# A two-layer transformer block on one core: the last batch gets its stacks in other memory

## The reference

```python
x = x + tanh(g_xattn[0]) * L0_xattn(layernorm(x), ctx)   # stage X: 8 heads of 64, 512 keys from ctx
x = x + tanh(g_ffn[0])   * L0_ffn(layernorm(x))          # stage F: 16 heads of 8, 256 keys from x; plus MoE, top 2 of 8
x = x + tanh(g_xattn[1]) * L1_xattn(layernorm(x), ctx)   # stage B: 16 heads of 8, 512 keys from ctx
x = x + tanh(g_ffn[1])   * L1_ffn(layernorm(x))          # stage C: MoE, top 2 of 8
```

## Time and profile before

| | |
|---|---|
| median of 3 runs | 752.22 us (744.86, 756.33, 752.22) |
| the profiled execution's own time | 746.59 us |
| its span, first to last instruction | 744.8 us |
| mean granted clock of PE, as a share of full speed | 0.933 |
| busy: PE, DVE, ACT, POOL | 89%, 76%, 50%, 46% |

### The profile page before, as it was taken

How to read it: one execution, slowest core, us unless ns; L and a number is a source line. 1 busy time by engine, 2 the same in 40 slices (tenths; PEclk the granted TensorE clock), 3 DMA queues, 4 the chain that set the end, 5 groups by cost and what they waited for, 6 DMA issues and landing times.

```text
span 744.8 us, 13302 instructions
## 1 busy us (share of the span) xinstructions
PE 663.1 (89%) x5232; PEld 336.2 (45%) x5232; DVE 569.7 (76%) x1055; ACT 374.2 (50%) x482; POOL 344.5 (46%) x467
## 2 busy tenths in 40 slices
PE   6699898998999899989999999989999789787684
PEld 2265454553544455434645355534653424333342
DVE  2626578589998879788898979887888987928534
ACT  4064345545546753775357644765357346263360
POOL 4273753852463257415663368326764324422233
PEclk9599999999999999989999999999999969969597
DMA  7210202112101221121121311121013221021000
GB/s 193 80 58 19 86 1 62 45 44 63 43 24 41 77 64 52 52 79 32 41 66 42 99 48 65 36 75 50 22 58 97 71 68 68 4 89 55 7 1 14
DMA packets 45790, 40.82 MB, mean 55 GB/s; under 512 B 4824, under 2 KB 37536, under 8 KB 45728
## 3 DMA queue, kind: packets, MB, share of 16 engines
q1 hardware_dynamic: 45168, 39.52, 17.1%
q10 hardware_dynamic: 560, 0.46, 0.2%
HBM read 22.93 MB, written 17.04 MB: 54 GB/s over the span
## 4 chain that ended last, share of the span: by engine, by line
PE 66%; DVE 21%; ACT 6%; issue 2%; POOL 2%; DMA 2%; SPq 1%; POOLq 0%; DVEq 0%
PE psum L670 13%; PE psum L626 7%; PE psum L590 7%; DVE mx8B L925 7%; PE psum L582 6%; DVE mxA L831 4%; PE psum L658 4%; ACT probB L740 4%; PE psum L557 3%; PE psum L639 3%; PE psum L551 3%; PE psum L600 2%; PE psum L577 2%; DVE rden L839 2%; PE psum L675 2%
## 5 line engine op out<-in xcount | busy, mean ns | idle before, releaser
L925 DVE TENSOR_REDUCE mx8B<-psum 128x2 f32<-128x1024 f32 x128 | 153.7, 1219 | 22.7 <-PE psum L639 21.5
L740 ACT ACTIVATE probB<-psum 128x1024 f32<-128x1024 f32 x128 | 126.4, 1029 | 57.2 <-PE psum L658 56.5
L727 ACT ACTIVATE probX<-psum 128x1024 f32<-128x1024 f32 x64 | 65.5, 1024 | 95.1 <-PE psum L582 94.8
L920 DVE TENSOR_REDUCE mx8F<-psum 128x4 f32<-128x1024 f32 x64 | 77.0, 1217 | 8.8 <-PE psum L633 8.6
L831 DVE TENSOR_REDUCE mxA<-psum 128x2 f32<-128x1024 f32 x64 | 76.6, 1216 | 8.5 <-PE psum L564 8.1
L839 DVE RECIPROCAL rden<-psum 128x256 f32<-128x256 f32 x32 | 56.1, 1752 | 34.8 <-PE psum L594 34.7
L740 ACT ACTIVATE probF<-psum 128x1024 f32<-128x1024 f32 x64 | 65.1, 1026 | 24.0 <-PE psum L658 22.2
L999 POOL TENSOR_TENSOR prodC<-prodC 128x256 f32<-128x256 f32 x30 | 21.8, 725 | 104.6 <-DVE prodC L913 102.3
L670 PE MATMUL psum<-probB,v8B 128*32 128x256 f32 x1024 | 67.5, 408 | 2.8 <-ACT probB L740 2.7
L582 PE MATMUL psum<-qX,kX 64*128 64x256 f32 x512 | 68.4, 388 | 0.0
L991 POOL TENSOR_TENSOR psum_k<-probX 128x512 f32<-128x512 f32 x32 | 40.8, 1274 | 59.5 <-ACT probX L727 58.5
(11 more groups left out here) (192 smaller groups left out, 1174.2 us busy)
## 6 DMA issues: line engine op xcount, KB each, us to landing
k8B<-k_dK SPq DMA_DIRECT2D x32, 192.0 KB
k_dK<-partsK SPq DMA_DIRECT2D x8, 384.0 KB, 2.5
q8F<-q_dF SPq DMA_DIRECT2D x32, 96.0 KB
k8F<-k_dF SPq DMA_DIRECT2D x32, 96.0 KB
q8B<-q_dB SPq DMA_DIRECT2D x32, 96.0 KB
k_dK<-partsK SPq DMA_DIRECT2D x8, 256.0 KB, 2.7
cTX<-in_ctxT SPq DMA_DIRECT2D x8, 192.0 KB, 2.8
cTK<-in_ctxT SPq DMA_DIRECT2D x8, 192.0 KB, 2.4
```

What stands on the lines that cost most here:

```text
L727: nc.scalar.activation(prob[s][(8 * b + k) % SLOTS[s]][:], ps, ACT.Exp, scale=float(XD) ** -0.5).then_inc(done["ACT"], 1)
L740: nc.scalar.activation(prob[s][(units * b + k) % SLOTS[s]][:], ps, ACT.Exp, scale=float(D8) ** -0.5).then_inc(done["ACT"], 1)
L920: nc.vector.tensor_reduce(mx8[s][:].rearrange("p t (i q) -> p i t q", i=2)[:, :, :, k], ps.rearrange("p (i t n) -> p i t n", i=2, t=QT), A ...
L925: nc.vector.tensor_reduce(mx8[s][:, t, :].rearrange("p (i q) -> p i q", i=2)[:, :, p], ps.rearrange("p (i n) -> p i n", i=2), AX.X, ALU.ma ...
```

## The change

For the last batch (7) alone:

- K's keys and values are made from `cTX`, the context that stage X loaded for the same batch. The load into `cTK` falls away.
- The queries of B go to `q8F` in place of `q8B`. The first half of the keys goes to `k8F` and the second half to `kXb`. These are free when F's exps and X's maxima of batch 7 are done. The reads into them wait for F's last exp, no longer for B's exps of batch 6.
- POOL sets `kXb` to 1.0 first, in a new job `ones`, for the rows that stay 1.0.
- `mr` of batch 7 doesn't wait for the exps of batch 6.

The way in which the maxima are sent and read (L512, L517) is the same before and after. In the diff, the helper functions `queries`, `keys` and `context` name the new places.

```diff
+LAST = BATCH - 1
@@ plan_stack
+    if s == "K" and b == LAST:
+        p.job("POOL", s, "ones", b, 0, 2.2, ("PE", "X", "mx", b, 7))
     for k in range(2):
-        p.job("SP", s, "sr", b, k, 2.6 if s == "F" else 1.3, ("SP", s, "sw", b, 0), ("PE", *old, b - 1, (4 if s == "F" else 8) * k + 3 + 4 * (s != "F")))
+        free = ("PE", *old, b - 1, (4 if s == "F" else 8) * k + 3 + 4 * (s != "F"))
+        if s != "F" and b == LAST:
+            free = ("POOL", "K", "ones", b, 0) if s == "K" and k else ("PE", "F", "e8", b, NPAIR - 1)
+        p.job("SP", s, "sr", b, k, 2.6 if s == "F" else 1.3, ("SP", s, "sw", b, 0), free)
@@ plan_attend
-    p.job("SP", s, "mr", b, 0, 1.25, ("SP", s, "mw", b, 0), ("PE", s, "e8", b - 1, units - 1))
+    p.job("SP", s, "mr", b, 0, 1.25, ("SP", s, "mw", b, 0), *[("PE", s, "e8", b - 1, units - 1)] * ((s, b) != ("B", LAST)))
@@ plan_k
+def context(b):
+    return "K" if b < LAST else "X"
-    p.job("SP", "K", "ctx", b, 0, .4, ("PE", "K", "kk", b - 1, 0), ("PE", "K", "vv", b - 1, 1))
-    p.fill("ACT", 0, "K", "kk", b, 0, 1.0, 1.4, [("SP", "K", "ctx", b, 0)], [("SP", "K", "sw", b - 1, 0)])
+    if b < LAST:
+        p.job("SP", "K", "ctx", b, 0, .4, ("PE", "K", "kk", b - 1, 0), ("PE", "K", "vv", b - 1, 1))
+    p.fill("ACT", 0, "K", "kk", b, 0, 1.0, 1.4, [("SP", context(b), "ctx", b, 0)], [("SP", "K", "sw", b - 1, 0)])
@@ build
+        def queries(s, b):
+            return q8["F" if (s, b) == ("B", LAST) else s]
+        def keys(s, b, rows, p):
+            if (s, b) != ("B", LAST):
+                return k8[s][rows, p, :]
+            if p < NPAIR // 2:
+                return k8["F"][rows, 2 * p:2 * p + 2, :].rearrange("r o n -> r (o n)")
+            return kXb[rows, p - NPAIR // 2, :]
@@ load_parts
-                sp.wait_ge(*is_full(to, "e8", b - 1, NPAIR * KEYS[to] // SEQ // 2 * (k + 1) - 1))
+                if (to, b) != ("B", LAST):
+                    sp.wait_ge(*is_full(to, "e8", b - 1, NPAIR * KEYS[to] // SEQ // 2 * (k + 1) - 1))
+                else:
+                    sp.wait_ge(*is_full("F", "e8", LAST, NPAIR - 1))
+                    if s == "K" and k:
+                        sp.wait_ge(padded, 1)
@@ mr
-                    sp.wait_ge(*is_full(s, "e8", b - 1, NPAIR * KEYS[s] // SEQ - 1))
+                    if (s, b) != ("B", LAST):
+                        sp.wait_ge(*is_full(s, "e8", b - 1, NPAIR * KEYS[s] // SEQ - 1))
@@ pool
+                if name == "ones":
+                    pool.wait_ge(*is_full("X", "mx", b, 7))
+                    engine.memset(kXb[:], 1.0).then_inc(padded, 1)
```

More of the change, by code:

```diff
@@ L149, in plan_f @@
                 [("DVE", "F", "wb", b, 0), ("POOL", "B", "xb", b - 1, 0), ("DVE", "B", "xh", b - 1, 0)])
+def context(b):
+    return "K" if b < LAST else "X"
 def plan_k(p, b):
-    p.job("SP", "K", "ctx", b, 0, .4, ("PE", "K", "kk", b - 1, 0), ("PE", "K", "vv", b - 1, 1))
-    p.fill("ACT", 0, "K", "kk", b, 0, 1.0, 1.4, [("SP", "K", "ctx", b, 0)], [("SP", "K", "sw", b - 1, 0)])
+    if b < LAST:
+        p.job("SP", "K", "ctx", b, 0, .4, ("PE", "K", "kk", b - 1, 0), ("PE", "K", "vv", b - 1, 1))
+    p.fill("ACT", 0, "K", "kk", b, 0, 1.0, 1.4, [("SP", context(b), "ctx", b, 0)], [("SP", "K", "sw", b - 1, 0)])
     plan_stack(p, "K", b, 3.9, 3, ("ACT", "K", "kk", b, 0), ("B", "e8"))
     for k in range(2):
-        p.fill("DVE", 0, "K", "vv", b, k, .58, .43, [("SP", "K", "ctx", b, 0)], [("PE", "B", "pv8", b - 1, 3)])
+        p.fill("DVE", 0, "K", "vv", b, k, .58, .43, [("SP", context(b), "ctx", b, 0)], [("PE", "B", "pv8", b - 1, 3)])
 def plan_b(p, b):
@@ L403, in build @@
         w_keys, w_values, w_queries, w_ident, zeroed = sem("w_keys"), sem("w_values"), sem("w_queries"), sem("w_ident"), sem("zeroed")
-        picked = sem("picked")
+        picked, padded = sem("picked"), sem("padded")
         def bank(s, name, b, k):
@@ L482, in load_parts @@
                     if s != "K":
-                        engine.dma_start(q8[s][rows, pairs, :].rearrange("r p n -> r (p n)"),
+                        engine.dma_start(queries(s, b)[rows, pairs, :].rearrange("r p n -> r (p n)"),
                                          q_d[s].rearrange("j (i d p) n -> i d j p n", i=2, p=NPAIR)[i, :, :, pairs]
@@ L486, in load_parts @@
                     if s != "B":
-                        engine.dma_start(k8[to][rows, pairs, :].rearrange("r p n -> r (p n)"),
+                        stack = k8[to][rows, pairs, :]
+                        if (to, b) == ("B", LAST):
+                            stack = kXb[rows, :, :] if k else k8["F"][rows, :, :]
+                        engine.dma_start(stack.rearrange("r p n -> r (p n)"),
                                          k_d[s].rearrange("j (i d p) n -> i d j p n", i=2, p=NPAIR)[i, :, :, pairs]
@@ L514, in _ @@
                     sp.wait_ge(*after(s, "mw", b))
-                    sp.wait_ge(*is_full(s, "e8", b - 1, NPAIR * KEYS[s] // SEQ - 1))
+                    if (s, b) != ("B", LAST):
+                        sp.wait_ge(*is_full(s, "e8", b - 1, NPAIR * KEYS[s] // SEQ - 1))
                     for i in range(2):
-                        engine.dma_start(q8[s][64 * i + KROWS:64 * i + MROWS],
+                        engine.dma_start(queries(s, b)[64 * i + KROWS:64 * i + MROWS],
                                          m2_d[s].rearrange("t (i p) n -> i t p n", i=2)[i]).then_inc(S[s]["mr"], 16)
@@ L607, in _ @@
                 elif name == "kk":
-                    pe.wait_ge(*after("K", "ctx", b))
-                    last = mm(ps[:, 0:KV], wk8["B"][:], cT["K"][:, :], start=True, stop=True)
+                    pe.wait_ge(*after(context(b), "ctx", b))
+                    last = mm(ps[:, 0:KV], wk8["B"][:], cT[context(b)][:, :], start=True, stop=True)
                 elif name in ("v8", "vv"):
@@ L613, in _ @@
                     else:
-                        pe.wait_ge(*after("K", "ctx", b))
+                        pe.wait_ge(*after(context(b), "ctx", b))
                     for j in range(2):
                         c = 2 * k + j
-                        tok = xT["F"][:, c * P:(c + 1) * P] if s == "F" else cT["K"][:, c * P:(c + 1) * P]
+                        tok = xT["F"][:, c * P:(c + 1) * P] if s == "F" else cT[context(b)][:, c * P:(c + 1) * P]
                         last = mm(ps[:, j * P:(j + 1) * P], tok, wv8["F" if s == "F" else "B"][:], start=True, stop=True)
@@ L638, in _ @@
                         for i in range(2):
-                            last = mm(ps[:, KV * i:KV * (i + 1)], q8[s][64 * i:64 * i + KROWS, p, t * P:(t + 1) * P],
-                                      k8[s][64 * i:64 * i + KROWS, p, :], start=True, stop=True)
+                            last = mm(ps[:, KV * i:KV * (i + 1)], queries(s, b)[64 * i:64 * i + KROWS, p, t * P:(t + 1) * P],
+                                      keys(s, b, slice(64 * i, 64 * i + KROWS), p), start=True, stop=True)
                 elif name == "mT8":
@@ L658, in _ @@
                             last = mm(ps[:, 512 * i + SEQ * c:512 * i + SEQ * (c + 1)],
-                                      k8[s][64 * i:64 * i + MROWS, p, (c0 + c) * P:(c0 + c + 1) * P],
-                                      q8[s][64 * i:64 * i + MROWS, p, :], start=True, stop=True)
+                                      keys(s, b, slice(64 * i, 64 * i + MROWS), p)[:, (c0 + c) * P:(c0 + c + 1) * P],
+                                      queries(s, b)[64 * i:64 * i + MROWS, p, :], start=True, stop=True)
                 elif name == "pv8":
@@ L964, in _ @@
                     made = True
-                if name == "rs":
+                if name == "ones":
+                    pool.wait_ge(*is_full("X", "mx", b, 7))
+                    engine.memset(kXb[:], 1.0).then_inc(padded, 1)
+                elif name == "rs":
                     pool.wait_ge(*after(s, "mv", b))
```

## The result

The changed kernel takes 764.69 us (median of 4 runs, 763.27 to 765.50); the kernel before takes 749.75 (4 runs, 744.86 to 756.33). The ratio is 1.0162, with a 95% interval of 1.0119 to 1.0205: slower, and the interval reaches just past 2%. The quotient of the two medians is 1.020, and against the 25 later runs of the kernel before (median 753.69, beside E1 to E4) it is 1.015, so the size is known to about half a per cent. The forecast was 762.8 us, and slower by 1.4%.

A forecast was written before the change was run, and what follows sets the result against it. Bound by PE's work from 400 to 560 us, later by the chain inside stage B. Batch 4's milestone 562.0 + periods 116.0 + end 75.1 = 753.1, plus clock 2.3 = 755.4 us of span; median 762.8, range 750 to 775.

The forecast's parts named there:

- The order as the cost: Middle of the program: B's jobs lose priority to X and F from batch 2 on, putting batch 4's milestone 25.5 us late.
- batch 4's lateness: Batch 4's milestone (second copy of `mT8` on DVE) moves from 536.5 to 562.0 us, and later milestones follow.
- X's end: X's last output, 559.5 us before, comes 2.5 us later because F's gate instructions move between `pv` of X's batch 7.
- The periods: From batch 4's milestone to batch 6's: kept at 62.0 + 54.0 = 116.0 us, with ends 87.4 and 124.
- Rival 4: A faster kernel: both periods shrink to 43.7 us, giving 734.2 us as median; chance 0.06.
- Rival 1: Cold end and long periods: all eight `pv8` blocks cold, both periods 62.0 us, giving 777.7 us as median; chance 0.24.
- The end: From batch 6's milestone to the program's end: 75.1 us in place of 92.3.
- The clock: PE's granted clock near the end: two more cold `pv8` blocks, 2.3 us, with 0 and 9.2 as ends.
- The base: Forecast span 755.4 us, 10.6 more; profiled execution 746.6 becomes 757.2, and the median lies 5.6 higher, at 762.8.
- The gain of 17.2 us: Program's end: batch 7's maxima run beside batch 6's HBM way and exps, cutting 92.3 us to 75.1.
- Rival 3: The order costs less: X's end stays, both periods 54.0 us, the clock costs nothing, 750.0 us as median; chance 0.16.
- Rival 2: Stack reads hang behind F's last exp or in SP's queue; the end stays 92.3 us, median 777.7; chance 0.04.

The follow-up runs named there:

- E1: Kernel before, its lists ranked by the changed plan's priorities, with old dependencies, places and waits: 779.41 us, ratio to before 1.0360.
- E4: Changed kernel, with one planner line letting the transpose of batch 4's maxima start without the allowance for drains queued on DVE: 756.63 us, ratio 1.0065.
- E5: Kernel before, with one planner dependency more: the transpose of batch 4's maxima comes behind X's output of batch 7: 783.12 us, ratio 1.0429.
- E11: Changed kernel, with the planner's allowance for queued drains (`LEAD`) at 1.75 in place of 2.0: 761.79 us, ratio 1.0122.
- E2: New places and waits with the lists of the kernel before (one `cTK` load out, the memset in): 751.20 us, ratio 0.9959.
- E7: Changed kernel, with batch 7's keys and values made from their own load of the context again: 763.29 us.
- E8: Changed kernel, with the two matmuls of each of stage B's maxima of batches 5 to 7 issued twice: 766.74 us.
- E3: Changed kernel, with jobs ranked by the old plan, so lists stay as before up to about 600 us: 758.73 us, ratio 1.0063.
- E10: Changed kernel with the old plan's ranks, and batch 7's stage B maxima taken up to half a microsecond early: 753.91 us, ratio 1.0009.
- E9: Kernel before, with the transpose of X's batch 6 maxima behind B's 14th maximum of batch 3: 790.35 us, median of three; a fourth took 967.24.
- E6: Changed kernel with the old plan's ranks, and the transpose of batch 4's maxima behind X's output of batch 7: 778.63 us.
- run 25: A count, not a label: the kernel before, unchanged, executed 25 times beside E1 to E4: median 753.69 us, 745.85 to 759.33.

## Why the prediction was right, and where it was off

The prediction held in direction, in size (1.4% against 1.62%) and in the two parts of its mechanism, a cost of the order and a gain at the end. The terms behind these parts were less good, and the sum came out better than it deserved.

**The order as the cost.** Right. E1 has the order without the places and is 25.7 us slower than before; the prediction's term was 25.5 us. That they agree so well is luck: between the two profiled executions it is 31.4 us (776.2 against 744.8). E4 gives back 8 us by a line that moves one transpose, and E5 makes the kernel before slower by the same move. But the prediction carried batch 4's lateness on one for one, and that is no rule here: at F's end 17 us of it became 7.5 in E4, 16 became 2.6 in E11, and 28 became 36 in E5. E2 shows that the places, the memset and the waits cost nothing.

**X's end, "I take 2.5 us, with 0 and 6 as ends".** Mis-sized: it measured 7.7. From batch 3's milestone (455.7 us before, 455.1 after) X's last output took 104.2 us before and 111.9 after. It took 111.8, 111.3, 112.0 and 114.0 us in E1, E4, E7 and E8, which have the new list there (E4 nearly to the end of it), and 104.5, 104.0 and 104.3 in E2, E3 and E10, which have the old. The price is clear of this scatter, but I had put it on the gate's instructions. They added 1.5 us between the second and third `oTX` of batch 7 on DVE (5.3 to 6.8 us), and the next `oTX` came 3.7 us sooner behind. The lag was there already at X's first maximum of batch 7 (23.3 us behind batch 3's milestone before, 30.4 after). In PE's list seven of the eight exps of X's batch 6 stood ahead of the transpose of B's batch 3, and now only one does: the output of X's batch 6 comes 29 us later.

```profile
504.51 0.48 DVE L878 SCALAR_TENSOR_TENSOR x<-psum,gates,xbX 128x256 f32<-128x256 f32 x1 [0.66 <-PE psum L633]
```

Before, that row began at 475.51. I compared the lists near the one place and not ahead of it. That the move of batch 6 causes the lag was not shown by an experiment of its own: E9 was to do it and has no usable profile.

**The periods, 116.0 us.** They were 58.6 + 61.5 = 120.1 us, inside the ends of 87.4 and 124. Rival 4, which needed short periods, didn't come. PE and DVE were busy for 97.5 and 87.1 of 119.8 us (the first two windows above), so that neither was full; I take it that the chain of B's own steps set them, which no run here tests. A second cause stands beside it, untested as well: PE's granted clock was 0.87 and 0.78 in these windows, against 0.93 and 0.85 in the two of before. Rival 1, with periods of 124 and eight cold blocks, didn't come either: there was one cold block.

**The end, 75.1 us.** It measured 76.4. The first exps of batch 6 wait for batch 7's maxima in PE's list: ACT takes them one by one at 692.16, 693.89, 696.04, 697.77 and 699.50 us.

**The clock, "two more cold blocks than before".** Wrong in sign. Of the eight blocks of `pv8` of batches 6 and 7, two were cold before (3.13 us and 3.64 us at 705.64), and after only one (3.10 us at 699.88, shown above), because the two bursts of exps became one. The low clock lies where DVE is the bound: 0.66 from 686.8 to 709.9 us (0.50, the lower level, up to 702), and 0.88 after. The Trainium skill's rule in "TensorE: Matmul & The Clock Gate", section "HAM oscillation — how this bites in real kernels", is that each burst behind a wait begins slow. The traces agree for the first block of each burst of batches 6 and 7 (3.13, 3.64 and 3.10 us, against 1.91 to 1.98 for the others), and I drew the wrong end from it: with one burst less there was one cold start less. This counts the blocks alone; the lower clock in the two periods is outside the term.

**The base.** Span against span, I forecast 10.6 us and it was 18.3; the terms above are 4.6, 4.1 and 1.3 us of it, less the 2.3 for the clock, which the blocks don't show. That the median came within 2 us is partly luck. I added 5.6 us for the median over the profiled execution, and the changed kernel's profiled execution lies at its median.

**The gain of 17.2 us.** The step "the stacks of batch 7 no longer wait for batch 6's exps, a gain of 17.2 us" gave the right sum for this list, since batch 6 is 18.7 us behind F. As a statement on the change it was wrong: E2, E3 and E6 show that it isn't there in lists where batch 6 is only 3.5 us behind. The places repair a delay that the new list makes.

Rival 3 (a cheap order) and rival 4 fell with E1. Rival 2 (stacks late) was not true as a cause of delay, but its idea, that the reads hang behind F's batch 7, points at the stretch that has nearly the same length in all kernels with new places.

No kernel here is clearly faster than the kernel before. E2 (751.20) is the best, at 0.9959 of before, and its interval takes in 1.

## What to carry to other kernels

When a planner sets the order, a dependency that is taken away at the end can change priorities in the middle of the program, as here. Test the two apart: the new lists with the old dependencies, and the old lists with the new ones. A gain counted from one milestone must be counted again from the milestone of the other input: here the keys came early and the queries, which hang on F, did not. Compare the lists from their first difference on, not only around the place where the loss shows. And when two profiles are compared, look first at the stretch in which their lists are the same: what differs there is not the edit.

## What was unexpected of the hardware

Whole executions of one program differ by up to 13 us: the kernel before, run 25 times beside E1 to E4, took 745.85 to 759.33 us. The traces show one place where this comes from. E2 and E3 have the same lists up to about 600 us. Their second milestone (batch 1) is at 294.0 and 294.2 us, but batch 3's is at 457.9 and 465.2. From 294 to 456 us PE's granted clock is 1.00 in E2 and 0.96 in E3. Distances between milestones repeat better where the clock is the same: from batch 3's milestone to X's last output it took 111.9, 111.8 and 112.0 us in three kernels with the same list there. In E8, with this list too, it took 114.0 us, and the granted clock from 540 to 567 us was 0.87, against 1.00 in the changed kernel. So in this kernel a difference of some microseconds in one profile says little by itself, and a distance between milestones says more only with the clock beside it.

More matmuls in a stretch didn't raise its granted clock: 87.0 us busy of 100 with a clock of 0.78, against 79.0 with 0.79 (E8).
